# Four in-order instruction streams of a chunk of a selective scan, laid out in another order

## The chip, the cores and the metric

One Trainium2 chip, one NeuronCore of it. The metric is the device time of one execution in microseconds (us); smaller is better. Before the change it is 11698.7 us, the median of 3 runs (11697.71 to 11724.16).

## The reference

A batch of 8 images (96 channels, 64x64) goes through a Mamba-like block with a convolutional branch, then through linear attention and a quantised feed-forward layer. The part that matters here is the selective scan, over 4 directions `k`, 192 channels `d` and 16 states `n`, along the 4096 positions of an image:

```python
x_dbl = jnp.einsum('bkdl,kcd->bkcl', xs, x_proj_w)
dts, bs, cs = (x_dbl[:, :, :R], x_dbl[:, :, R:R + N], x_dbl[:, :, R + N:])
dts = jnp.einsum('bkrl,kdr->bkdl', dts, dt_projs_w)
delta = jax.nn.softplus(dts + dt_projs_b[None, :, :, None])
...
dA = jnp.exp(dt_i[..., None] * A)
hst = dA * hst + (dt_i * u_i)[..., None] * b_i[:, :, None, :]
y = jnp.einsum('bkdn,bkn->bkd', hst, c_i)
```

## The kernel before

Three phases run one after the other: `phase_inputs` (line 70), `phase_scan` (line 379) and `phase_outputs` (line 1163). The change is in `phase_scan` alone.

**Tiling.** The scan walks 8 images x 4 directions x 4 chunks of 1024 positions: 128 chunks. The 192 x 16 states of a chunk are 24 tiles of 128 partitions x 1024 positions, numbered 0 to 23 (`i` in the code). For each tile, four things happen:

- ScalarE makes the decay, exp(A * delta), with `expo` (line 893). It reads `rep`, delta copied to 128 partitions.
- The drive, delta * u * B, comes from one of two places. For 18 tiles GpSimd multiplies it (`drive`, line 1108) into a ring of four buffers `dBu`; a drive has a number of its own, `place(i)`, from 0 to 17. For the 6 "turned" tiles 9 to 14 ScalarE scales delta * u, turned so that positions lie on partitions (`scale_du`, line 934, 32 small steps in a chunk), and TensorE turns it back (`turn_back`, line 799, 8 blocks of 128x128).
- VectorE runs the recurrence (`scan`, line 1068). 16 tiles ("kept") are scanned into one of 8 buffers `h`; the other 8 (0, 3, 4, 6, 15, 18, 19, 21) are scanned in place in the PSUM buffer `pd`.
- The states are multiplied by C: kept tiles by GpSimd (`weigh`, line 1116), the others by VectorE (`weigh`, line 1077). TensorE then sums three tiles at a time into `py` (`reduce_states` j sums tiles 3j to 3j+2, line 821). After groups 0 to 3 ScalarE copies the first half of y out of `py` (`copy_y(n, 0)`, line 968), and after groups 4 to 7 the second half (`copy_y(n, 1)`). The first sum of the next half waits for that copy.

Beside this, the chunk's delta and delta * u of the next chunk are made, in two halves of 96 channels: TensorE's `make_step` (L767), ScalarE's `absolute`, `exp_abs`, `relu`, `one_plus`, `log` (L940 to L958), TensorE's `add_up` (L775 to L780), which adds up the four parts of softplus, ScalarE's `copy_delta` (L963), VectorE's `delta_u` (L1049), TensorE's `turn_du` (L787) and ScalarE's `copy_du` (L921). For the chunk after the next, TensorE's `make_x_dbl` (L749) and `turn_b` (L757) and ScalarE's `copy_x_dbl` (L910) and `copy_b` (L914) make B and C. All of these share one PSUM buffer, `pp`.

**What sets the order.** Every engine runs its own list, in order, written out by hand: `body` for TensorE, VectorE and GpSimd, and on ScalarE `run` (line 1000), which goes through steps i = 0 to 23. At each step it saves the last column of a state for the next chunk (`save_state`, L901), issues `expo(i + 2)`, and then what the tables `STEPS`, `SCALE` (scaling steps of this chunk) and `SCALE_NEXT` (of the next one) put there. `copy_y` and `copy_x_dbl` have their steps in the code. A `pd` buffer is free for `expo(i)` when tile i - 2 has been scanned, or, if it is scanned in place, weighed. SP's list of DMAs waits for semaphores of all four engines.

Of the kernel before, what the change touches and what calls it, by code (L numbers as in the profile page):

```python
# [378 lines left out]
def phase_scan(nc, a):  # L379

    with ExitStack() as ctx:
# [358 lines left out]
        def _(pe):  # L740
# [95 lines left out]

            def body(bk, k, c, left):
                n, s = bk * NC + c, c % 2
                reduce_states(n, k, 0)
                if left:  # L840
                    add_up(n + 1, 0)
                turn_back(bk, c, 9)
                turn_back(bk, c, 10)
                reduce_states(n, k, 1)
                turn_back(bk, c, 11)
                turn_back(bk, c, 12)
                if left:
                    turn_du(n + 1, 0)
                turn_back(bk, c, 13)
                if left:  # L850
                    make_step(n + 1, 1)
                turn_back(bk, c, 14)
                skip(n, s, 0)
                reduce_states(n, k, 2)
                reduce_states(n, k, 3)
                reduce_states(n, k, 4)
                if left:
                    add_up(n + 1, 1)
                skip(n, s, 1)
                if left:  # L860
                    turn_du(n + 1, 1)
                reduce_states(n, k, 5)
                if left >= 2:
                    make_x_dbl(n + 2, s)
                    turn_b(n + 2)
                    make_step(n + 2, 0)
                reduce_states(n, k, 6)
                reduce_states(n, k, 7)
# [3 lines left out]
        def _(act):  # L872
# [107 lines left out]
            for i in range(2):  # L980
# [4 lines left out]

            STEPS = {1: [(absolute, 0)],
                     2: [(exp_abs, 0), (relu, 0), (one_plus, 0)],
                     4: [(log, 0)],
                     8: [(copy_delta, 0)],
                     11: [(copy_du, 0)],  # L990
                     12: [(absolute, 1), (exp_abs, 1)],
                     13: [(relu, 1)],
                     14: [(one_plus, 1)],
                     16: [(log, 1)],
                     18: [(copy_delta, 1)],
                     20: [(copy_du, 1)]}
            SCALE = {0: 3, 2: 2, 3: 3, 4: 2, 5: 6, 6: 2, 7: 1}
            SCALE_NEXT = {20: 5, 21: 3, 22: 2, 23: 3}

            def run(bk, k, c, left, first, span):  # L1000
                n, s = bk * NC + c, c % 2
                for i in span:
                    if c < NC - 1:
                        for q in range(NS):
                            if SAVED_AT[q] == i:
                                save_state(bk, k, c, q)
                    if i + 2 < NS:
                        expo(bk, k, c, i + 2)
                    elif left:
                        if c == NC - 1 and i + 2 == NS:  # L1010
                            pick_a(bk + 1, (k + 1) % K)
                        expo(*((bk, k, c + 1) if c < NC - 1 else (bk + 1, (k + 1) % K, 0)), i + 2 - NS)
                    if i == 2 and not first:
                        copy_y(n - 1, 1)
                    if i == 14:
                        copy_y(n, 0)
                    if left:
                        for step, half in STEPS.get(i, ()):
                            step(n + 1, half)
                        if left >= 2 and i == 22:  # L1020
                            copy_x_dbl(n + 2)
                        if left >= 2 and i == 23:
                            copy_b(n + 2, s)
                    if i in SCALE:
                        made = AHEAD + sum(SCALE[q] for q in SCALE if q < i)
                        scale_du(n, s, made, made + SCALE[i])
                    if left and i in SCALE_NEXT:
                        made = sum(SCALE_NEXT[q] for q in SCALE_NEXT if q < i)
                        scale_du(n + 1, 1 - s, made, made + SCALE_NEXT[i])

# [10 lines left out]
        def _(dve):  # L1041
# [43 lines left out]
            def body(bk, k, c, left):  # L1085
                n, s = bk * NC + c, c % 2
                for j in range(8):
                    for i in range(3 * j, 3 * j + 3):
                        scan(bk, k, c, i)
                        if not is_kept(i):  # L1090
                            weigh(n, i)
                        if left and i in (10, 20):
                            delta_u(n + 1, 1 - s, (10, 20).index(i))
            chunk_loop(dve, body)

        @block.gpsimd
        def _(pool):
# [24 lines left out]
            def body(bk, k, c, left):  # L1122
                n = bk * NC + c
                drive(n, c, 3)
                drive(n, c, 4)
                weigh(n, k, 1)
                weigh(n, k, 2)
                drive(n, c, 5)
                drive(n, c, 6)
                drive(n, c, 7)  # L1130
                drive(n, c, 8)
# [11 lines left out]
                weigh(n, k, 14)  # L1143
                drive(n, c, 12)
                drive(n, c, 13)
                weigh(n, k, 16)
                weigh(n, k, 17)
                drive(n, c, 14)
                drive(n, c, 15)
                drive(n, c, 16)  # L1150
                drive(n, c, 17)
# [759 lines left out]
```

## Time and profile before

| | |
|---|---|
| median of 3 runs | 11698.7 us |
| the profiled execution: its own time | 11687.62 us |
| span of the profile, first to last instruction | 11685.8 us |
| `phase_scan`, about 838 to 10117 us of the span | 9279 us, 128 chunks |
| the chunk that is read below, from its first scan to that of the next | 5050.18 to 5122.46 us, 72.28 us |
| mean granted TensorE clock | 0.871 of 2.4 GHz |
| busy share of the whole span | TensorE 79%, VectorE 86%, ScalarE 72%, GpSimd 75% |

In the rows, PE is TensorE (PEld its weight loads), DVE is VectorE, ACT is ScalarE, POOL is GpSimd and SP the DMA queue's engine. A row of a timeline has a start, a duration, the engine, the line of the kernel, the operation and its tiles; "xN" is a run of N like instructions, "[idle before <-releaser]" how long the engine stood idle ahead of it and which event ended that. Lines are those of the kernel before; in the kernel after they are the same up to the table `STEPS` (line 986) and lie one lower behind it.

### The profile page before, as it was taken

Reading aid. Unit: us, or ns where it says so; the run is one execution under the profiler, and the core shown is the slowest. Engines: PE = TensorE matmul, PEld = TensorE weight load, DVE = VectorE, ACT = ScalarE, POOL = GpSimd, SP = SyncE. Lnnn points to the kernel's source line nnn. Section 1 sums busy time; section 2 is a strip of 40 time slices with the busy share of each in tenths; the row PEclk is TensorE's granted clock in tenths of the full one; section 3 lists DMA queues with packets and bytes.
Section 4 is the critical chain, followed back from the end, with each engine's and each line's share of the span. In section 5 each row is a group of like instructions: output and inputs, shape, how many; then the busy total and the mean of one; then the engine's idle time right before and its main releaser. Section 6 shows DMA issues by size and latency. Waiting matters only on the chain. (4 is left out here: it accounts for less than half of the span.)

```text
span 11685.8 us, 144402 instructions
## 1 busy us (share of the span) xinstructions
PE 9207.4 (79%) x34584; PEld 3443.5 (29%) x34584; DVE 10036.1 (86%) x6335; ACT 8437.5 (72%) x13829; POOL 8772.1 (75%) x4468
## 2 busy tenths in 40 slices
PE   8877777777777777777777777777777777588888
PEld 2322222222222222222222222222222222233333
DVE  7759999999899989999999899999999999866565
ACT  6767777777777777777777777777777777455555
POOL 0019999899899989999999899999999999521210
PEclk9988888888888888888888888888888888799999
DMA  3347777787777777777777777777777777643441
GB/s 103 122 127 185 183 187 184 178 187 186 183 180 185 187 183 181 186 187 183 184 185 188 179 183 185 185 182 181 185 186 184 187 186 182 149 112 94 100 108 49
DMA packets 577596, 1948.45 MB, mean 167 GB/s; under 512 B 106614, under 2 KB 111638, under 8 KB 562198
## 3 DMA queue, kind: packets, MB, share of 16 engines
q1 hardware_dynamic: 573714, 1938.65, 69.8%
q8 instruction: 272, 4.46, 0.2%
q14 instruction: 534, 4.37, 0.1%
q10 hardware_dynamic: 3076, 0.97, 0.1%
HBM read 1532.38 MB, written 406.85 MB: 166 GB/s over the span
## 5 line engine op out<-in xcount | busy, mean ns | idle before, releaser
L1108 POOL TENSOR_TENSOR dBu<-rep,shared 128x1024 f32<-128x1024 f32 x2304 | 4552.5, 1998 | 886.2 <-DMA rep<-dd_dram 833.5
L1116 POOL TENSOR_TENSOR h<-h,shared 128x1024 f32<-128x1024 f32 x2048 | 4020.7, 1972 | 728.6 <-DVE h L1068 728.0
L893 ACT ACTIVATE pd<-rep,a_now 128x1024 f32<-128x1024 f32 x2304 | 2556.1, 1109 | 362.7 <-DVE h L1068 200.9
L821 PE MATMUL py<-h,fold 128*32 128x512 f32 x8192 | 2447.8, 701 | 214.9 <-ACT y L968 214.9
L1068 DVE TENSOR_TENSOR_SCAN h<-pd,carry,dBu 128x1024 f32<-128x1024 f32 x960 | 2242.4, 2344 | 409.7 <-ACT pd L893 280.0
L1068 DVE TENSOR_TENSOR_SCAN pd<-pd,carry,dBu 128x1024 f32<-128x1024 f32 x768 | 1795.8, 2338 | 0.1
L821 PE MATMUL py<-shared,fold 128*32 128x512 f32 x3072 | 1479.6, 880 | 221.8 <-ACT y L968 173.3
L934 ACT ACTIVATE shared<-shared,turned_b 128x192 f32<-128x192 f32 x4096 | 1553.2, 442 | 15.5 <-ACT shared L921 5.4
L799 PE MATMUL pd<-eye,shared 128*128 128x128 f32 x6144 | 1006.9, 316 | 619.3 <-DVE h L1068 466.9
L1068 DVE TENSOR_TENSOR_SCAN h<-h,carry,pd 128x1024 f32<-128x1024 f32 x576 | 1308.8, 2326 | 43.2 <-PE pd L799 32.3
L799 PEld LDWEIGHTS pd<-eye,shared 128*128 128x128 f32 x6144 | 792.8, 159 | 1083.4 <-DVE h L1068 478.0
L1077 DVE TENSOR_TENSOR shared<-pd,shared 128x1024 f32<-128x1024 f32 x768 | 940.5, 1225 | 87.8 <-DVE pd L1068 26.0
L893 ACT ACTIVATE h<-rep,a_now 128x1024 f32<-128x1024 f32 x768 | 867.4, 1140 | 1.2 <-PE py L821 1.2
L1068 DVE TENSOR_TENSOR_SCAN h<-pd,dBu 128x1024 f32<-128x1024 f32 x320 | 729.2, 2284 | 139.5 <-ACT pd L893 88.7
L1813 POOL TENSOR_TENSOR shared<-shared 96x1024 f32<-96x1024 f32 x56 | 139.2, 2516 | 938.9 <-DMA shared<-y_dram 938.9
L767 PE MATMUL pp<-xdbl,w_dt 38*96 38x512 f32 x1024 | 716.8, 836 | 152.0 <-ACT turned_b L914 151.1
L787 PE MATMUL pp<-eye,RL 96*128 96x96 f32 x2048 | 298.1, 307 | 559.5 <-DVE RL L1049 554.5
L821 PEld LDWEIGHTS py<-h,fold 128*32 128x32 f32 x8192 | 484.4, 124 | 567.3 <-issue 531.4
L1068 DVE TENSOR_TENSOR_SCAN pd<-pd,dBu 128x1024 f32<-128x1024 f32 x256 | 585.4, 2287 | 66.0 <-ACT pd L893 50.2
L775 PE MATMUL pp<-W,neg 97*96 97x512 f32 x1024 | 545.5, 614 | 106.5 <-ACT W L953 106.5
L921 ACT ACTIVATE shared<-pp 128x768 f32<-128x768 f32 x256 | 207.5, 810 | 571.1 <-PE pp L787 571.1
L968 ACT ACTIVATE y<-py 96x1024 f32<-96x1024 f32 x256 | 260.7, 1019 | 473.1 <-PE py L821 473.0
(174 smaller groups left out, 14120.2 us busy)
## 6 DMA issues: line engine op xcount, KB each, us to landing
rep<-dd_dram SPq DMA_DIRECT2D x1024, 768.0 KB, 13.0
shared<-bc_dram SPq DMA_DIRECT2D x3584, 128.0 KB, 4.6
u<-u_dram SPq DMA_DIRECT2D x128, 768.0 KB, 6.8
dd_dram<-LG SPq DMA_DIRECT2D x256, 384.0 KB, 4.0
dd_dram<-RL SPq DMA_DIRECT2D x256, 384.0 KB, 5.1
y_dram<-y SPq DMA_DIRECT2D x256, 384.0 KB, 8.1
shared<-y_dram SPq DMA_DIRECT2D x63, 1536.0 KB, 15.7
u_dram<-shared SPq DMA_DIRECT2D x32, 1536.0 KB, 7.5
```

Of the source, the lines that this page charges most:

```text
L767: last = mm(pp[0:HALF, t2(t)], w_dt[:, half * HALF:(half + 1) * HALF], xdbl[:, t2(t)], start=True, stop=True)
L775: mm(pp[0:HALF, t2(t)], neg[:, :], W1[:, t2(t)], start=True, stop=False)
L787: last = nc.tensor.transpose(pp[:, q * 128:q * 128 + HALF], du[:, block_of(q)], eye)
L799: last = nc.tensor.transpose(pd[:, i % 2, block_of(q)], turned_dbu[:, q, half * 3 + g, :, :], eye128[:, :])
L821: last = mm(py[32 * g:32 * g + 32, t2(t)], fold[:, :], weighted(3 * j + g, k)[:, t2(t)], start=(j % 4 == 0), stop=(j % 4 == 3), skip_group ...
L893: go(dst, rep[:, half, 0, g, :], ACT.Exp, scale=a_now[:, column(i)]).then_inc(S.exped, 1)
L934: go(turned_dbu[:, q, :, j, :], turned_du[:, q, :, :], ACT.Identity, scale=turned_b[:, s, q, j:j + 1]).then_inc(S.scaled, 1)
L968: go(y[:, :], py[0:HALF, :], ACT.Identity).then_inc(S.y_made, 1)
L1068: v.tensor_tensor_scan(turned(state(i, k), k), turned(decay, k), turned(drive, k), first, ALU.mult, ALU.add).then_inc(S.scanned, 1)
L1077: v.tensor_tensor(weighted(i, 0), pd[:, i % 2, :], CC[:, r, :], ALU.mult).then_inc(S.hc_dve, 1)
L1108: nc.gpsimd.tensor_tensor(dBu[:, ring(c, p), :], rep[:, half, 1, g, :], BB[:, r, :], ALU.mult).then_inc(S.dbu, 1)
L1116: nc.gpsimd.tensor_tensor(turned(weighted(i, k), k), turned(kept(i, k), k), turned(CC[:, r, :], k), ALU.mult).then_inc(S.hc_pool, 1)
```

## The change

Nothing is added or removed: the same instructions with the same waits stand in another order on TensorE, ScalarE, VectorE and GpSimd.

```diff
@@ body of TensorE
                 n, s = bk * NC + c, c % 2
-                reduce_states(n, k, 0)
                 if left:
                     add_up(n + 1, 0)
                 turn_back(bk, c, 9)
+                reduce_states(n, k, 0)
                 turn_back(bk, c, 10)
+                turn_back(bk, c, 11)
                 reduce_states(n, k, 1)
-                turn_back(bk, c, 11)
-                turn_back(bk, c, 12)
                 if left:
                     turn_du(n + 1, 0)
+                turn_back(bk, c, 12)
                 turn_back(bk, c, 13)
...
                 reduce_states(n, k, 3)
-                reduce_states(n, k, 4)
                 if left:
                     add_up(n + 1, 1)
+                reduce_states(n, k, 4)
                 skip(n, s, 1)
@@ ScalarE
             STEPS = {1: [(absolute, 0)],
                      2: [(exp_abs, 0), (relu, 0), (one_plus, 0)],
-                     4: [(log, 0)],
-                     8: [(copy_delta, 0)],
+                     5: [(log, 0)],
+                     7: [(copy_delta, 0)],
                      11: [(copy_du, 0)],
-                     12: [(absolute, 1), (exp_abs, 1)],
-                     13: [(relu, 1)],
-                     14: [(one_plus, 1)],
-                     16: [(log, 1)],
+                     12: [(absolute, 1)],
+                     13: [(exp_abs, 1), (relu, 1), (one_plus, 1)],
+                     15: [(log, 1)],
                      18: [(copy_delta, 1)],
                      20: [(copy_du, 1)]}
-            SCALE = {0: 3, 2: 2, 3: 3, 4: 2, 5: 6, 6: 2, 7: 1}
-            SCALE_NEXT = {20: 5, 21: 3, 22: 2, 23: 3}
+            SCALE = {0: 3, 1: 1, 2: 3, 3: 1, 4: 2, 5: 5, 6: 4}
+            SCALE_NEXT = {20: 3, 21: 2, 22: 4, 23: 4}
...
-                    if i == 2 and not first:
+                    if i == 4 and not first:
                         copy_y(n - 1, 1)
-                    if i == 14:
+                    if i == 16:
                         copy_y(n, 0)
...
-                        if left >= 2 and i == 22:
+                        if left >= 2 and i == 23:
                             copy_x_dbl(n + 2)
@@ body of VectorE
-                        if left and i in (10, 20):
-                            delta_u(n + 1, 1 - s, (10, 20).index(i))
+                        if left and i in (9, 20):
+                            delta_u(n + 1, 1 - s, (9, 20).index(i))
@@ body of GpSimd
                 drive(n, c, 3)
+                weigh(n, k, 1)
                 drive(n, c, 4)
-                weigh(n, k, 1)
+                drive(n, c, 5)
                 weigh(n, k, 2)
-                drive(n, c, 5)
...
                 drive(n, c, 13)
+                drive(n, c, 14)
                 weigh(n, k, 16)
                 weigh(n, k, 17)
-                drive(n, c, 14)
```

Three places, as the two programs have them. First ScalarE in steps 2 to 4 of a chunk. Before, the copy of y (L968) stands between the exponential of tile 4, just above these rows, and that of tile 5 (the last row):

```order
L967 ISA
L968 ACTIVATE y<-py 96x1024
L944 ACTIVATE E<-E 96x1024
L947 ISA
L949 ACTIVATE RL<-pp,b_dt 96x1024
L953 ACTIVATE W<-E 96x1024
L934 ACTIVATE shared<-shared,turned_b 128x6x32 x2
L901 ACTIVATE carry<-h 128x1
L900 REGISTER_ALU
L901 ACTIVATE carry<-pd 128x1
L903 REGISTER_ALU
L893 ACTIVATE pd<-rep,a_now 128x1024
```

Now, from the first save of step 3 on (L893 is the exponential of tile 5, then that of tile 6):

```order
L900 REGISTER_ALU
L901 ACTIVATE carry<-pd 128x1
L903 REGISTER_ALU
L893 ACTIVATE pd<-rep,a_now 128x1024
L934 ACTIVATE shared<-shared,turned_b 128x6x32
L901 ACTIVATE carry<-h 128x1
L900 REGISTER_ALU
L901 ACTIVATE carry<-pd 128x1
L903 REGISTER_ALU
L893 ACTIVATE pd<-rep,a_now 128x1024
L967 ISA
L968 ACTIVATE y<-py 96x1024
```

The copy of y has moved behind the exponentials of tiles 5 and 6, and one scaling step more (L934) stands ahead of tile 5's.

Second, ScalarE where one chunk passes into the next (L893 is the exponential of the next chunk's tile 0, then that of its tile 1; L901 saves states). Before:

```order
L893 ACTIVATE pd<-rep,a_now 128x1024
L906 REGISTER_ALU
L907 ISA
L908 ISA
L910 ACTIVATE xdbl<-pp 38x1024
L934 ACTIVATE shared<-shared,turned_b 128x6x32 x2
L901 ACTIVATE carry<-h 128x1
L898 REGISTER_ALU
L901 ACTIVATE carry<-h 128x1
L893 ACTIVATE pd<-rep,a_now 128x1024
L914 ACTIVATE turned_b<-pp 128x32
L933 REGISTER_ALU
```

Now:

```order
L893 ACTIVATE pd<-rep,a_now 128x1024
L934 ACTIVATE shared<-shared,turned_b 128x6x32
L933 ISA
L934 ACTIVATE shared<-shared,turned_b 128x6x32 x3
L901 ACTIVATE carry<-h 128x1
L898 REGISTER_ALU
L901 ACTIVATE carry<-h 128x1
L893 ACTIVATE pd<-rep,a_now 128x1024
L906 REGISTER_ALU
L907 ISA
L908 ISA
L910 ACTIVATE xdbl<-pp 38x1024
```

The copy of x_dbl (L910) has moved behind tile 1's exponential, with four scaling steps ahead of that instead of two.

Third, TensorE between turn 9 (the last of its eight blocks is the first row) and group 1's sum. Before, with group 0's sum done earlier still, ahead of `add_up`:

```order
L799 MATMUL pd<-eye,shared 128x128
L793 REGISTER_ALU
L799 MATMUL pd<-eye,shared 128x128 x8
L818 REGISTER_ALU x2
L816 REGISTER_ALU
L821 MATMUL py<-shared,fold 32x512 x2
L821 MATMUL py<-h,fold 32x512
L821 MATMUL py<-shared,fold 32x512 x2
L821 MATMUL py<-h,fold 32x512
L793 REGISTER_ALU
L799 MATMUL pd<-eye,shared 128x128 x8
```

Now:

```order
L799 MATMUL pd<-eye,shared 128x128
L818 ISA
L816 ISA
L816 REGISTER_ALU
L821 MATMUL py<-shared,fold 32x512
L821 MATMUL py<-h,fold 32x512 x2
L821 MATMUL py<-shared,fold 32x512
L821 MATMUL py<-h,fold 32x512 x2
L793 REGISTER_ALU
L799 MATMUL pd<-eye,shared 128x128 x8
L793 REGISTER_ALU
L799 MATMUL pd<-eye,shared 128x128 x8
```

Group 0's sum now stands between turns 9 and 10, and turn 11 follows turn 10 ahead of group 1's sum.

## Rows read from the trace of the kernel before

**Rows 1.** Busy time by stretch: PE, PEld, DVE, ACT, POOL, clock, DMA.

```profile
5050.18:5122.46 72.28, 56.81 (x226) 21.56 (x224) 66.82 (x35) 55.66 (x98) 66.02 (x35) 0.86 0.79 186
...
5077.30:5085.00 7.70, 7.50 (x31) 4.01 (x32) 7.60 (x4) 7.22 (x13) 7.70 (x5) 0.56 0.34 93
5085.00:5095.00 10.00, 9.10 (x57) 5.36 (x57) 9.63 (x6) 5.68 (x8) 7.78 (x5) 1.00 0.72 171
...
838.00:10117.00 9279.00, 7198.57 (x28587) 2709.70 (x28585) 8492.41 (x4350) 7032.94 (x11789) 8497.67 (x4350) 0.86 0.78 183
```

**Rows 2.** What VectorE waited for, 3000 to 7000 us: total, times, longest.

```profile
DVE h L1068 <- ACT pd L893: 148.8, 103, 4.3
DVE h L1068 <- POOL dBu L1108: 58.0, 34, 3.6
DVE pd L1068 <- ACT pd L893: 37.1, 7, 7.7
```

**Rows 3.** Timeline of VectorE, 5050 to 5122.5 us.

```profile
5047.91 2.35 DVE L1068 TENSOR_TENSOR_SCAN h<-pd,carry,dBu 128x1024 f32<-128x1024 f32 x1 [0.33 <-ACT pd L893]
...
5054.30 4.69 DVE L1068 TENSOR_TENSOR_SCAN h<-pd,carry,dBu 128x1024 f32<-128x1024 f32 x2 [0.33 <-ACT pd L893]
...
5068.99 2.35 DVE L1068 TENSOR_TENSOR_SCAN h<-pd,carry,dBu 128x1024 f32<-128x1024 f32 x1 [2.88 <-ACT pd L893]
...
5085.81 9.06 DVE L1068 TENSOR_TENSOR_SCAN h<-h,carry,pd 128x1024 f32<-128x1024 f32 x4 [0.37 <-PE pd L799]
...
5101.25 2.35 DVE L1068 TENSOR_TENSOR_SCAN h<-pd,carry,dBu 128x1024 f32<-128x1024 f32 x1 [0.52 <-ACT carry L901]
...
5120.20 2.35 DVE L1068 TENSOR_TENSOR_SCAN h<-pd,carry,dBu 128x1024 f32<-128x1024 f32 x1 [0.33 <-ACT pd L893]
```

**Rows 4.** Timeline of ScalarE, 5045 to 5125 us.

```profile
5051.02 1.02 ACT L910 ACTIVATE xdbl<-pp 38x1024 f32<-38x1024 f32 x1 [1.31 <-PE pp L749]
...
5052.82 1.10 ACT L893 ACTIVATE pd<-rep,a_now 128x1024 f32<-128x1024 f32 x1
5053.86 0.18 ACT L914 ACTIVATE turned_b<-pp 128x32 f32<-128x32 f32 x1
...
5055.16 1.12 ACT L893 ACTIVATE pd<-rep,a_now 128x1024 f32<-128x1024 f32 x1
...
5059.28 1.10 ACT L893 ACTIVATE pd<-rep,a_now 128x1024 f32<-128x1024 f32 x1
5062.72 1.02 ACT L968 ACTIVATE y<-py 96x1024 f32<-96x1024 f32 x1 [2.34 <-PE py L821]
5063.64 1.04 ACT L944 ACTIVATE E<-E 96x1024 f32<-96x1024 f32 x1
...
5067.51 1.12 ACT L893 ACTIVATE pd<-rep,a_now 128x1024 f32<-128x1024 f32 x1
```

**Rows 5.** Timeline of TensorE, 5046 to 5122.5 us.

```profile
5052.18 0.66 PE L757 MATMUL pp<-eye,xdbl 38*128 38x38 f32 x8 [1.41 <-ACT xdbl L910]
...
5061.99 0.59 PE L821 MATMUL py<-h,fold 128*32 128x512 f32 x2
...
5072.02 1.96 PE L780 MATMUL pp<-LG,eye 96*96 96x512 f32 x4
5077.33 1.75 PE L799 MATMUL pd<-eye,shared 128*128 128x128 f32 x7 [3.35 <-DVE h L1068]
5079.23 2.46 PE L799 MATMUL pd<-eye,shared 128*128 128x128 f32 x9
5081.62 1.07 PE L821 MATMUL py<-shared,fold 128*32 128x512 f32 x2
...
5082.48 1.07 PE L821 MATMUL py<-shared,fold 128*32 128x512 f32 x2
...
5088.21 1.09 PE L799 MATMUL pd<-eye,shared 128*128 128x128 f32 x8 [0.90 <-DVE h L1068]
```

**Rows 6.** Timeline of GpSimd, 5045 to 5122.5 us.

```profile
5061.14 7.89 POOL L1108 TENSOR_TENSOR dBu<-rep,shared 128x1024 f32<-128x1024 f32 x4
```

## The prediction

> **What bounds the kernel now.** I read four views in this order. First the busy time by stretch, to see which engine is near its limit in the scan phase. It lasts 9279 us for 128 chunks, 72.5 us each, and VectorE and GpSimd are busy in 8492 and 8498 us of it, that is 66.3 and 66.4 us a chunk; in the chunk that I walk through, 66.82 and 66.02 of 72.28 us [rows 1]. TensorE and ScalarE have over 15 us of room. So no engine is full: two engines at 92% stand still some 6 us a chunk, and each of these waits can only be repaired by what ends it.
>
> Second, what VectorE waited for between 3000 and 7000 us, which is 55 chunks: most of it goes to the exponentials on ScalarE, 148.8 + 37.1 us, and 58.0 us are put down to GpSimd's drives [rows 2]. The second name is not to be trusted: a wait for several semaphores goes to the one whose last update came latest, whoever it was for. The timeline tells more. In the chunk from 5050.18 us VectorE has one long stall, 2.88 us ahead of tile 5, and short ones of 0.33 (tile 1), 0.37 (tile 11), 0.52 (tile 17) and 0.33 us (tile 23) [rows 3]; the other 1.0 us are small hand-overs, as from a scan in PSUM to its own product, which no order changes. (The row from 5054.30 us holds the scans of tiles 1 and 2, 2.25 us apart.)
>
> Third, why tile 5 waits. ScalarE made tile 4's exponential at 5059.28, then waited 2.34 us for TensorE with the copy of y's second half, did it at 5062.72, then three parts of softplus and two scaling steps, and came to tile 5's exponential at 5067.51; the scan began 1.48 us behind that start, just as tile 1's scan began 1.48 us behind its own (5052.82 and 5054.30) [rows 3, 4]. Nothing on VectorE's side needed the copy at that moment: the exponentials are queued behind it because ScalarE runs its list in order.
>
> Fourth, TensorE: it finished group 7's sum at 5062.58 (5061.99 + 0.59), which released the copy [rows 5].
>
> **The change part by part.** Times are from the first scan of a chunk, t = 0 at 5050.18.
>
> *The copy of y's second half behind tile 6's exponential.* It leaves the path to tile 5 with its wait and its own 0.92 us (5062.72 to 5063.64). At its new place, about t = 18, group 7 has been summed for 5 us, so it waits for nothing. Who waits for it: group 0's sum on TensorE, which is moved behind `add_up` and turn 9 for that, and SP's store of y.
>
> *The chunk's start.* The copy of x_dbl moves from in front of tile 1's exponential to behind it. That exponential needs the scan of tile 23, over at t = 0.08 (5047.91 + 2.35) [rows 3], and can start at about 0.8, when ScalarE has done four scaling steps behind tile 0's exponential, instead of 2.64. Tile 1 then loses its stall of 0.33: its scan starts at 3.8. But the copy of x_dbl starts at 0.8 + 1.03 = 1.85, 1.0 later than before. The turn of B starts 1.16 behind that and takes 0.66 [rows 4, 5], so the copy of B comes at 3.9 instead of 3.68. Between it and tile 2's exponential there were three scaling steps and 1.30 us; now there are four, at 0.35 each (3 of them took 1.13 with an overlap): 5.5 instead of 4.98. Tile 2 is scanned at 5.5 + 1.48 = 7.0; before it was 6.37, right behind tile 1. So this part costs 0.6 us at tile 2, between 0 (if the copy of B is ready early) and 1.2 (if TensorE's x_dbl is late by as much again).
>
> *Up to tile 5.* From tile 2's exponential to tile 4's it was 4.10 us; with one scaling step more 4.47: t = 10.0. Then, without the copy, 1.03 for itself and 3.87 + 0.35 for what stood between 5063.64 and 5067.51, again with one scaling step more: tile 5's exponential at 15.2, its scan at 16.7. VectorE itself gets there 9.56 us behind tile 2's scan (5056.55 to 5068.99, less the stall of 2.88), at 16.6, so a stall of about 0.1 is left of 2.88. The scan stood at 18.81: **2.1 us gained**, with 0.6 of loss already in it.
>
> *Tiles 6 to 9.* The log (step 5), five and four scaling steps stand between the exponentials of tiles 7, 8 and 9. Added up at the same paces, tile 8's is just in time and tile 9's 0.35 late. I take **0.35 lost**, between 0 and 0.7.
>
> *Turns ahead of sums, and delta * u after tile 9.* Turn 9 needs the last scaling step, which comes at about 9.3 us behind tile 5's scan. So it ends at 26.3, and group 0's sum, four rounds that start 0.43 apart at the full clock, at 28.2. Turn 10 ends at 29.4. Tile 10 needs it at 30.8, since delta * u (1.12 us) now stands ahead of tile 10 and covers it: 1.1 us of margin with 0.3 for the hand-over. Turn 11 follows as soon as tile 9 is scanned, so the 0.37 us at tile 11 go. Turn 12 now stands behind group 1 and the turn of delta * u and has 0.1 to 0.3 us of margin at the full clock. **0.37 gained**; the lower end is the third rival below.
>
> *The copy of y's first half behind tile 18's exponential:* tile 17 no longer waits for a save and an exponential queued behind it. **0.52 gained**. Ahead of tile 23's exponential five scaling steps become three, 0.7 us, so its stall of 0.33 goes. **0.33 gained**.
>
> *At nothing.* `add_up` of the second half ahead of group 4's sum: both lie in TensorE's room. GpSimd's product of tile 1 ahead of drive 4 makes it idle about 1 us (drive 3 is over at 5.2, tile 1 is scanned at 6.1), but drive 4 is still ready at about 10 for a scan at 12.9. Drive 14 two places earlier has its ring buffer by then and lets SP load B and u earlier. If this cover is gone, the price is that of the fourth rival.
>
> Sum for this chunk: 2.1 - 0.35 + 0.37 + 0.52 + 0.33 = 2.97, so 3.0 us of 72.28. Over 128 chunks 384 us; the phases before and after are untouched. Against the profiled execution's own 11687.6 us that is 11304 us; the median of the runs is 11 us above it, so I forecast **11310 us**. A measurement of this kernel can tell about 0.3%, 35 us or 0.27 us a chunk, from no change.
>
> **A rule against it.** The rows show both clocks around the turns: a mean of 0.56 of 2.4 GHz, nearly all at 1.2, in the 7.7 us that begin with turns 9 and 10 after 3.35 us without work, and 1.00 in the next 10 us with turns 11 to 14 [rows 1, 5]. The Trainium skill ("TensorE: Matmul & The Clock Gate", Part 4, PE-mode transpose) says that the high clock does not engage for transposes, which don't count as work in the same way. By that rule a stretch with more turns in a row would stay at 1.2 GHz, and the third or fifth rival would come out. In the trace turns 11 to 14 ran at the full clock between other matmuls, so I give the rule a small part. The Trainium skill ("GPSIMD Engine Reference", Key points) also says that GpSimd contends with VectorE's instructions of two SBUF inputs; that would make it slower as VectorE's gaps close. The row says no: four drives took 7.89 us, 1.97 each, though VectorE stood idle in 2.88 us of them [rows 3, 6], and over the phase its 4350 instructions take 1.95 us each [rows 1].
>
> **The rivals.**
>
> *Second, the chunk's start costs nothing* (chance 0.11). ScalarE catches up, and the stalls go with no new ones at tiles 2 and 9: 2.88 + 0.33 + 0.37 + 0.52 + 0.33 = 4.4, less 0.3 for hand-overs, 4.1 us: 525 us, 11175. For it: the sum of ScalarE's work is the same and it has 16 us of room. Against: the copy of x_dbl hangs on TensorE's late end.
>
> *Third, TensorE is late at turn 10* (0.16). If the slow stretch still begins at turn 9 and lasts as long as now, group 0's sum takes 1.7 us more (rounds 0.86 apart instead of 0.43) and turn 10 1.1 more (2.2 against 1.09) [rows 5]; less the 1.1 of margin, tile 10 stalls 1.7 us. The gain is 1.3 us: 166 us, 11530. For it: this stretch was slow in the chunk shown. Against: the idle time ahead of turn 9, after the last part of `add_up` (5072.02), shrinks from 3.35 us to about 1.3, since the log moves back towards it.
>
> *Fourth, GpSimd becomes the bound* (0.05). It needs 66.0 us itself; of its 6.26 us of idle time the part that stems from VectorE's stall of 2.88 goes, 0.9 us come in ahead of tile 1's product, and if all the rest binds, the chunk takes 72.28 - 2.88 + 0.9 = 70.3 us: 2.0 us gained, 256 in all, 11440.
>
> *Fifth, slower* (0.05). The clock stays at 1.2 GHz from group 0's sum through turn 12. Two sums at 1.7 and three turns at 1.1 us more are 6.7 us; less 0.2 of margin at turn 12, VectorE stalls 6.5 us between tiles 10 and 12, which outweighs the gain of 3.0 by 3.5: 448 us, 12145. It decides from 3.2 us of lateness at turn 12 on, that is when the slow stretch outlasts turn 11. [...]
>
> *Sixth, the change doesn't do what it says* (0.03): the stall stays with the copy at its new step, because group 7's sum slides back as well: within 0.3% of 11699. It would have to slide 5 us.
>
> **How the numbers follow.** Forecast 0.60, the others as given. Faster by over 0.3%: 0.60 + 0.11 + 0.16 + 0.05 = 0.92; within: 0.03; slower: 0.05. The ends: with the start's cost at 0 and tile 9's at 0 the gain is 4.0 to 4.1 us, 11170; with 1.2 at tile 2 and half of the third rival's stall it is 2.97 - 0.6 - 0.85 = 1.5 us, 11510.
>
> **What would show it.** Chunks of about 69.3 us; tile 5's stall down from 2.9 to under 0.5 us; no wait of the copy of y's second half for TensorE; a new stall of about 1 us at tile 2 and a short one at tile 9; none at tiles 11, 17, 23; GpSimd's wait ahead of tile 5's product gone. I am wrong if VectorE stalls at tiles 10 to 12 behind turns, if GpSimd has no idle time left, or if chunks stay over 71.

## The result, and the profile after

| | before | after |
|---|---|---|
| median of 4 runs each, same chip | 11702.44 us | **11232.64 us** (11205.89 to 11255.03) |
| ratio | | **0.9594** (95%: 0.957 to 0.9619) |
| profiled execution, its own time | 11687.62 us | 11255.03 us |
| mean granted TensorE clock | 0.871 | 0.864 |

The change makes the kernel 470 us faster, 3.67 us a chunk. The forecast was 11310 us (388 us, 3.0 a chunk) in a range of 11170 to 11510.

Busy time by stretch, after (PE, PEld, DVE, ACT, POOL, clock, DMA share, GB/s). The first row is a chunk from its first scan to that of the next, the second the whole scan phase, then 4000 us in the middle (58 chunks, 55 in the kernel before), and two short stretches around turns 9 to 12:

```profile
5396.20:5464.29 68.09, 56.47 (x224) 20.88 (x222) 66.49 (x36) 55.74 (x100) 66.68 (x35) 0.85 0.83 190
839.00:9650.00 8811.00, 7241.98 (x28588) 2649.50 (x28586) 8453.70 (x4350) 7048.51 (x11790) 8488.62 (x4349) 0.86 0.83 193
3000.00:7000.00 4000.00, 3303.83 (x12984) 1206.50 (x12984) 3829.76 (x1972) 3197.82 (x5341) 3849.55 (x1972) 0.86 0.84 193
5421.00:5425.00 4.00, 4.00 (x21) 1.97 (x19) 3.95 (x2) 4.00 (x9) 4.00 (x3) 0.60 0.00 0
5425.00:5437.00 12.00, 11.73 (x74) 6.64 (x74) 12.00 (x7) 7.79 (x12) 12.00 (x7) 1.00 0.63 168
```

The gain lies in the scan phase: 9279 us [rows 1] became 8811, 468 us less. VectorE's idle time in that phase fell from 787 to 357 us (span less busy time), that is from 6.15 to 2.79 us a chunk. The other 39 us, 0.30 a chunk, come out of its busy time at the same 4350 instructions: back-to-back instructions overlap by some 0.1 us (a row "4.58 ... x2" holds two scans of 2.35), and more of them stand back to back now. The profiled execution as a whole is only 433 us shorter than the one before, since its output phase, which no edit touches, took 1603 us and not 1569 (1571 to 1593 in the other runs' traces). So that the medians differ by 470 us, nearly the scan phase's 468, is in part chance.

What VectorE waited for, 3000 to 7000 us, after (total, times, longest; before: [rows 2]):

```profile
DVE h L1067 <- ACT pd L893: 58.0, 62, 5.5
DVE hC L1076 <- DMA shared<-bc_dram: 12.0, 18, 1.4
DVE h L1067 <- PE pd L799: 11.3, 22, 1.1
DVE h L1067 <- POOL dBu L1107: 7.3, 11, 4.3
DVE pd L1067 <- ACT pd L893: 2.1, 4, 0.7
```

The waits for exponentials fell from 185.9 to 60.1 us, those put down to the drives from 58.0 to 9.1 (a row of 1.8 for `pd` is not shown), those for ScalarE's saves (`carry`, L901) from 24.0 to 2.3. GpSimd's drives had not become faster (1998 ns each before, 2000 after, over 2304 of them), so that name was indeed the wrong one. Nor do they run slower beside a VectorE that is busy in 96% of the time instead of 91 (3829.76 and 3649.02 of these 4000 us). The Trainium skill ("GPSIMD Engine Reference", Key points) tells of contention with VectorE's instructions of two SBUF inputs. It does not bear on this kernel, and the prediction was wrong to hold it against the row: every scan and product of VectorE reads one of its two large inputs from `pd` or `pp`, which lie in PSUM. So no run here tests that rule.

Timeline of VectorE, after, in the chunk from 5396.20 us (tile 2; tile 3's product; tile 5; tile 9; delta * u; tiles 10 to 14; tiles 16 and 17; tile 18):

```profile
5402.73 2.35 DVE L1067 TENSOR_TENSOR_SCAN h<-pd,carry,dBu 128x1024 f32<-128x1024 f32 x1 [0.47 <-ACT pd L893]
...
5407.45 1.22 DVE L1076 TENSOR_TENSOR shared<-pd,shared 128x1024 f32<-128x1024 f32 x1
...
5412.45 2.35 DVE L1067 TENSOR_TENSOR_SCAN h<-pd,carry,dBu 128x1024 f32<-128x1024 f32 x1 [0.24 <-POOL dBu L1107]
...
5423.05 2.35 DVE L1067 TENSOR_TENSOR_SCAN h<-h,carry,pd 128x1024 f32<-128x1024 f32 x1
5425.31 1.20 DVE L1048 TENSOR_TENSOR RL<-pp,u 96x1024 f32<-96x1024 f32 x1
5426.47 11.30 DVE L1067 TENSOR_TENSOR_SCAN h<-h,carry,pd 128x1024 f32<-128x1024 f32 x5
...
5441.28 4.58 DVE L1067 TENSOR_TENSOR_SCAN h<-pd,carry,dBu 128x1024 f32<-128x1024 f32 x2
5445.78 2.33 DVE L1067 TENSOR_TENSOR_SCAN pd<-pd,carry,dBu 128x1024 f32<-128x1024 f32 x1
```

Tile 5 waits 0.24 us where it waited 2.88 [rows 3], and its scan starts at t = 16.25 where it started at 18.81. Tile 2 has the new stall of the forecast, here 0.47. There is nothing at tiles 9, 11 and 17. GpSimd's wait ahead of tile 5's product is gone as forecast: 2.30 us on average before, 0.24 after.

ScalarE in the same chunk (copy of x_dbl, copy of B, exponentials of tiles 2 and 5, copies of y's second and first half):

```profile
5397.74 1.00 ACT L910 ACTIVATE xdbl<-pp 38x1024 f32<-38x1024 f32 x1
...
5399.59 0.20 ACT L914 ACTIVATE turned_b<-pp 128x32 f32<-128x32 f32 x1 [0.84 <-PE pp L757]
...
5401.25 1.12 ACT L893 ACTIVATE pd<-rep,a_now 128x1024 f32<-128x1024 f32 x1
...
5410.97 1.12 ACT L893 ACTIVATE pd<-rep,a_now 128x1024 f32<-128x1024 f32 x1
...
5413.69 1.00 ACT L968 ACTIVATE y<-py 96x1024 f32<-96x1024 f32 x1
...
5444.73 1.00 ACT L968 ACTIVATE y<-py 96x1024 f32<-96x1024 f32 x1
```

Neither copy of y waits; the second half's copy had waited 2.34 us [rows 4]. Nor does TensorE wait for a copy of y any more, where it had waited 176.5 us between 3000 and 7000 us. Against t = 0 at 5396.20, the copy of x_dbl starts at 1.54 (forecast 1.85), the copy of B at 3.39 (3.9) and tile 2's exponential at 5.05 (5.5). The copy of B waits 0.84 us for TensorE's turn, with nothing between it and the copy of x_dbl.

TensorE: turn 9 (8 blocks), the first and last round of group 0's sum, turns 10 and 11 (16 blocks):

```profile
5420.95 1.92 PE L799 MATMUL pd<-eye,shared 128*128 128x128 f32 x8
...
5422.80 1.07 PE L821 MATMUL py<-h,fold 128*32 128x512 f32 x2
...
5424.81 0.59 PE L821 MATMUL py<-h,fold 128*32 128x512 f32 x2
5425.34 1.97 PE L799 MATMUL pd<-eye,shared 128*128 128x128 f32 x16
```

Turn 9 took 1.92 us at a clock near 1.2 GHz; turns 10 and 11, eight blocks each, took 1.97 together at the granted clock of 1.00. The Trainium skill ("TensorE: Matmul & The Clock Gate", Part 4, PE-mode transpose) says that the high clock does not engage for transposes; the trace does not agree, as far as these 16 go, which ran at it behind a sum that had already risen to it (its first rounds 0.86 apart, its last 0.43). Whether a stretch of nothing but transposes would rise to it no run shows.

Some chunks, most of them the second of a direction (13 of the 14 of chunks 16 to 111 whose tile 2 waits over 2 us), have a long stall. TensorE, ScalarE and VectorE in the one from 5042.92 us (timeline of all engines):

```profile
5042.22 6.86 PE L749 MATMUL pp<-u,w_x 96*38 96x512 f32 x8 [2.69 <-DMA u<-u_dram]
...
5049.34 1.02 ACT L910 ACTIVATE xdbl<-pp 38x1024 f32<-38x1024 f32 x1 [4.62 <-PE pp L749]
...
5054.33 2.35 DVE L1067 TENSOR_TENSOR_SCAN h<-pd,carry,dBu 128x1024 f32<-128x1024 f32 x1 [5.38 <-ACT pd L893]
```

The load of u was issued at 5030.77 and let TensorE start 11.4 us later; it had stood 2.69 us, made x_dbl at 1.2 GHz (6.86 us, where it takes 3.65 in the chunk above), the copy of x_dbl waited 4.62 us and tile 2 was scanned 5.38 us late.

### The profile page after: what moved, and what is told of

Same layout as the page of the kernel before. It is cut to its first block and busy times, and to the rows that moved or that the text cites. A ratio compares the mean times of both kernels' runs of the same rounds, so it can differ in the third digit from the quotient of the medians.

```text
span 11253.2 us, 144402 instructions
## 1 busy us (share of the span) xinstructions
PE 9276.6 (82%) x34584; PEld 3385.5 (30%) x34584; DVE 10007.4 (89%) x6335; ACT 8454.9 (75%) x13829; POOL 8763.8 (78%) x4468
## 5 line engine op out<-in xcount | busy, mean ns | idle before, releaser
L893 ACT ACTIVATE pd<-rep,a_now 128x1024 f32<-128x1024 f32 x2304 | 2560.4, 1111 | 395.4 <-DVE h L1067 198.3
L821 PE MATMUL py<-h,fold 128*32 128x512 f32 x8192 | 2472.6, 720 | 6.0 <-ACT y L968 6.0
L934 ACT ACTIVATE shared<-shared,turned_b 128x192 f32<-128x192 f32 x4096 | 1552.6, 442 | 15.6 <-ACT shared L921 5.4
L821 PE MATMUL py<-shared,fold 128*32 128x512 f32 x3072 | 1457.0, 839 | 5.3 <-POOL h L1115 4.3
L799 PE MATMUL pd<-eye,shared 128*128 128x128 f32 x6144 | 903.7, 296 | 178.0 <-DVE h L1067 127.4
L799 PEld LDWEIGHTS pd<-eye,shared 128*128 128x128 f32 x6144 | 734.6, 150 | 618.7 <-DVE h L1067 341.2
L893 ACT ACTIVATE h<-rep,a_now 128x1024 f32<-128x1024 f32 x768 | 866.4, 1140 | 16.1 <-PE py L821 15.3
L780 PE MATMUL pp<-LG,eye 96*96 96x512 f32 x1024 | 598.7, 715 | 228.9 <-ACT LG L958 228.8
L767 PE MATMUL pp<-xdbl,w_dt 38*96 38x512 f32 x1024 | 641.3, 757 | 37.6 <-ACT turned_b L914 36.7
L749 PE MATMUL pp<-u,w_x 96*38 96x512 f32 x1024 | 521.1, 656 | 90.8 <-DMA u<-u_dram 79.5
```

What stands on the lines that cost most here:

```text
L749: last = mm(pp[0:XD, t2(t)], w_x[:, half, :], u[:, s, half, t2(t)], start=(half == 0), stop=(half == 1))
L767: last = mm(pp[0:HALF, t2(t)], w_dt[:, half * HALF:(half + 1) * HALF], xdbl[:, t2(t)], start=True, stop=True)
L780: last = mm(pp[0:HALF, t2(t)], eye, LG[:, t2(t)], start=False, stop=True)
L799: last = nc.tensor.transpose(pd[:, i % 2, block_of(q)], turned_dbu[:, q, half * 3 + g, :, :], eye128[:, :])
L821: last = mm(py[32 * g:32 * g + 32, t2(t)], fold[:, :], weighted(3 * j + g, k)[:, t2(t)], start=(j % 4 == 0), stop=(j % 4 == 3), skip_group ...
L893: go(dst, rep[:, half, 0, g, :], ACT.Exp, scale=a_now[:, column(i)]).then_inc(S.exped, 1)
```

## The experiments

Below, "mean idle" is the idle time ahead of an instruction averaged over 96 chunks of a run's trace (chunks 16 to 111), so it answers for more than one timeline does; the length of a chunk is the mean over the first 126. For the kernels before and after:

| mean idle ahead of, us | tile 1 | tile 2 | tile 5 | tile 9 | tile 10 | tile 11 | tile 15 | tile 17 | tile 23 | all of VectorE | chunk |
|---|---|---|---|---|---|---|---|---|---|---|---|
| before | 0.50 | 0.01 | 3.01 | 0.09 | 0.00 | 0.33 | 0.39 | 0.44 | 0.26 | 6.32 | 72.54 |
| after | 0.00 | 0.98 | 0.20 | 0.05 | 0.14 | 0.00 | 0.03 | 0.00 | 0.00 | 2.87 | 68.85 |

My theory: the gain comes from the copy of y's second half, which no longer holds up ScalarE's exponentials. The rival: it comes from TensorE's order, and the copies matter little. Ratios are to the kernel before on the same chip; after is 0.959.

**y2_back**: after, with this copy at its old step. The rest of the change stays, so this run also shows what the rest is worth without the late copy.

```diff
-                    if i == 4 and not first:
+                    if i == 2 and not first:
                         copy_y(n - 1, 1)
```

> The kernel after with one part undone: the copy of y's second half stands at step 2 again, in front of the exponentials of tiles 5 and 6. Theory (ScalarE's list queues tile 5's exponential behind a copy that waits for group 7's sum): the copy waits some 2 us again and takes 0.9, tile 5 stalls 2.9 to 3.2 us instead of 0.2, the chunk gets 2.9 us longer, 11600 us (ratio to before 0.991). Rival (ScalarE's spare time swallows the copy wherever it stands, the gain came from the turns and sums on TensorE): under 1 us a chunk, 11350 us or less.

Measured 11485.21 us, 0.9806 (0.979 to 0.9823), chunks of 70.83 us. Tile 5's mean idle is 3.09 again and the copy waits 1.92. But the small waits at tiles 2, 6 and 10 shrink, so that the copy's place is worth 2.0 us a chunk and not the 2.9 that tile 5 waits longer: VectorE's stall had served as slack for others. The time lies between what the theory (11600) and the rival (11350 or less) foretold: with the copy at its old step the rest of the change still gives 1.9% of the 4.1.

**y2_alone**: before, with nothing changed but this copy (step 2 to 4).

> The kernel before with the copy of y's second half at step 4, and nothing else. Theory (the other parts of the change are there to make room for the late copy): group 0's sum, first in TensorE's list, waits for the copy until about t = 18 and holds up add_up, turn 9 and copy_delta behind it; tile 5's stall goes, but 1 to 2 us come back at tiles 9 to 12, so the gain is 1 to 2 us a chunk, 11450 to 11570 us. Rival (the copy alone carries the gain): 2.9 us a chunk or more, 11330 us or less.

Measured 12034.43 us, **1.0271** (1.0254 to 1.0289): slower than before. Tile 5's stall is gone (0.01), and 3.83 us stand ahead of tile 9, 1.57 ahead of tile 17. TensorE in this run, the first rows of group 0's sum and `add_up`, then turns 9 and 10; behind them tile 9's scan on VectorE:

```profile
5528.49 1.06 PE L821 MATMUL py<-shared,fold 128*32 128x512 f32 x1 [6.20 <-ACT y L968]
...
5532.06 1.91 PE L775 MATMUL pp<-W,neg 97*96 97x512 f32 x2
...
5539.82 1.91 PE L799 MATMUL pd<-eye,shared 128*128 128x128 f32 x16
```

```profile
5540.90 4.58 DVE L1068 TENSOR_TENSOR_SCAN h<-h,carry,pd 128x1024 f32<-128x1024 f32 x2 [3.72 <-PE pd L799]
```

The copy ran at 5527.17, and group 0's sum, first in TensorE's old order, had to wait for it: 6.20 us idle. The sum then took 3.6 us (rounds 0.85 apart, the 1.2 GHz pace), `add_up` stands behind it and turn 9 behind that. In the waits between 3000 and 7000 us, TensorE's wait for the copies grew from 176.5 us in the kernel before to 408.4. Both had this kernel faster and neither was right: the copy and TensorE's order are one edit.

**pe_back**: after, with TensorE's whole list of before.

> The kernel after with TensorE's list of before (group 0's sum first, sums of groups 0, 1 and 4 ahead of turns and of add_up). Theory: group 0's sum waits for the copy of y until t = 18, add_up ends at 27 instead of 24.5, turn 9 at 29, tiles 9 and 11 stall 1 to 2 us together, 11360 to 11490 us. Rival (TensorE has 15 us of room in a chunk, its order does not matter): 11233 us within 35.

Measured 12265.18 us, **1.0475** (1.0457 to 1.0492), 775 us over what was expected. Tile 9 waits 3.89 us, delta * u after tile 20 waits 2.72, tile 2 1.64; TensorE's wait for the copies is 609.8 us. The next two runs split this.

**g0_back**: after, with group 0's sum alone back at the head of the list.

```diff
+                reduce_states(n, k, 0)
                 if left:
                     add_up(n + 1, 0)
                 turn_back(bk, c, 9)
-                reduce_states(n, k, 0)
```

> The kernel after with group 0's sum first in TensorE's list again, ahead of add_up, and nothing else undone. Theory (the sum waits for the late copy of y, TensorE stands idle and falls to 1.2 GHz, and add_up, turn 9 and the copy of delta queue behind it): tile 9 stalls about 4 us as with the whole list of before, 4 us a chunk, 11700 to 11800 us. Rival (the stall at tile 9 came from the order of turns and sums after turn 9): under 1 us a chunk, 11350 us or less.

Measured 11655.48 us, 0.9976 (0.9966 to 0.9987), a little under the 11700 to 11800 expected. The stall is the one foretold, tile 9 waits 3.74 us, but the small waits at tile 2, tile 10 and the product of tile 6 shrink by 0.6 together, so the chunk gets 3.5 us longer and not 4. So nearly all of the change's gain hangs on whether group 0's sum stands behind `add_up` and turn 9, once the copy is late. TensorE in the chunk from 5317.17 us, the start of that sum and turns 9 and 10:

```profile
5336.40 1.06 PE L821 MATMUL py<-shared,fold 128*32 128x512 f32 x1 [5.58 <-ACT y L968]
...
5346.89 1.91 PE L799 MATMUL pd<-eye,shared 128*128 128x128 f32 x16
```

**g4_back**: after, with group 4's sum alone back ahead of `add_up` of the second half.

```diff
                 reduce_states(n, k, 3)
+                reduce_states(n, k, 4)
                 if left:
                     add_up(n + 1, 1)
-                reduce_states(n, k, 4)
```

> The kernel after with group 4's sum ahead of the second add_up again, and nothing else undone. Theory (the sum waits for the copy of y's first half, which now stands at step 16; add_up, the copy of delta and delta * u queue behind it): a stall of 1.5 to 3 us ahead of the second delta * u, 11430 to 11600 us. Rival (TensorE has slack there, as the prediction costed it at nothing): 11233 us within 35.

Measured 11934.82 us, **1.0207** (1.0183 to 1.0231), far over the expectation. Rows of one chunk; TensorE's group 4, its x_dbl; ScalarE's copy of delta; SP's load of u; VectorE's delta * u and, in the next chunk, tile 2:

```profile
5381.57 3.38 PE L821 MATMUL py<-h,fold 128*32 128x512 f32 x12 [5.42 <-ACT y L968]
...
5400.08 5.32 PE L749 MATMUL pp<-u,w_x 96*38 96x512 f32 x8 [2.81 <-DMA u<-u_dram]
```

```profile
5392.04 1.02 ACT L963 ACTIVATE LG<-pp 96x1024 f32<-96x1024 f32 x1 [5.88 <-PE pp L780]
```

```profile
5393.96 0.33 SPq L618 DMA_DIRECT2D u<-u_dram  x1
```

```profile
5393.20 1.22 DVE L1048 TENSOR_TENSOR RL<-pp,u 96x1024 f32<-96x1024 f32 x1 [2.74 <-ACT LG L963]
...
5410.65 2.35 DVE L1067 TENSOR_TENSOR_SCAN h<-pd,carry,dBu 128x1024 f32<-128x1024 f32 x1 [2.29 <-ACT pd L893]
```

The sum waits for the copy of y's first half, 5.42 us, and runs at the 1.2 GHz pace, 3.38 us. It then strikes twice. `add_up` is late, so delta is, and VectorE waits with delta * u. And `skip`, the last reader of u, is late, so SP loads the next u late, TensorE waits 2.81 us for it and makes x_dbl in 5.32 us, and tile 2 of the next chunk is late. I had counted the first strike, at 1.5 to 3 us, and not the second. Mean idle: 3.51 us at delta * u, 2.89 at tile 2.

**xdbl_back**: after, with the copy of x_dbl back at step 22 (ahead of tile 1's exponential).

> The kernel after with the copy of x_dbl at step 22 again, in front of the exponential of the next chunk's tile 1 (scaling steps as after). Theory: that exponential waits for TensorE's x_dbl and for four scaling steps, tile 1 stalls about 1.5 to 2 us, tile 2's stall of 1.0 shrinks by a part, net 0.5 to 1.4 us a chunk, 11300 to 11410 us. Rival (only the time of the copy of B counts, and that comes as early or earlier): no change or faster, 11233 us within 35 or less.

Measured 11408.25 us, 0.9743 (0.9727 to 0.976), at the upper end of what was expected. Tile 2's mean idle falls from 0.98 to 0.27, but tile 1's is 1.82, and chunks take 70.08 us. The new place is worth 1.2 us a chunk beside the new table of scaling steps, which puts four of them ahead of tile 1's exponential and which this run keeps. That does not contradict the forecast's loss of 0.6 for the chunk's start, which was against the kernel before: there tile 2 was scanned at 6.56 on average, with the whole change at 6.99, in this run at 8.20.

**pool_back**: after, with GpSimd's list of before.

> The kernel after with GpSimd's list of before (drive 4 ahead of tile 1's product, drive 5 behind tile 2's, drive 14 behind the products of tiles 16 and 17). Theory (GpSimd has 2 us of idle time in a chunk and every drive is ready 2 us early): 11233 us within 35. Rival (drive 14 frees B's buffer for SP's loads and, behind them, the load of u, so x_dbl and tile 2 come later): 0.5 us a chunk or more, 11300 us or more; or the reverse, loads less bunched with u's, and faster by 35 us or more.

Measured 11214.68 us, 0.9599 (0.9583 to 0.9616): no difference from after, as expected. But the loads change, see the last section.

**y1_back**: after, with the copy of y's first half at its old step 14.

> The kernel after, with the copy of y's first half back at step 14 (behind tile 16's exponential) instead of 16. By my forecast's term for it, tile 17's stall returns: 0.5 us a chunk, 65 us, ratio 0.965. The run g4_back showed that groups 3 and 4 and the copy hang together: with the copy two steps earlier it waits for the sum of group 3 (in the kernel before 1.0 us on average), and as ScalarE is then also late for the exponentials of tiles 17 to 19, the price may be 1 us a chunk: 0.970. A rival: group 4's sum, which waits for this copy, stands behind add_up now and comes later anyway, so nothing changes: 0.959.

Measured 11218.56 us, 0.9602 (0.9585 to 0.962): no difference, as the rival had it, though for another reason. The copy did not wait, 0.06 us on average where in the kernel before it waited 1.01. TensorE sums groups 2 and 3 earlier now, against the chunk's first scan: group 3's last round ends at 44.7 us on average and in the kernel before at 47.4, while ScalarE comes to the copy only 1.8 us earlier. So tile 17's stall goes by either edit: with the copy back it is 0.04, and with TensorE's old order and the copy at step 16 (pe_back, g0_back) it is 0.00.

Then three attempts at a version that is faster still. **after_again** runs after beside them.

> The kernel after, once more beside the other three: 0.959 of the time before.

Measured 11206.8 us, 0.9588 (0.9575 to 0.9601). The same program gives other waits in this trace than in the one above: 51.5 us for exponentials instead of 60.1, and in a direction's second chunk 1.58 us at tile 2 instead of 2.51. So a change of waits of that size, between two traces, says nothing.

**fill**: after, with two scaling steps of step 23 between the copy of x_dbl and the copy of B, in the 0.84 us in which ScalarE waits for TensorE's turn.

```diff
-            SCALE_NEXT = {20: 3, 21: 2, 22: 4, 23: 4}
+            SCALE_NEXT = {20: 3, 21: 2, 22: 5, 23: 3}
...
+                        if i == 23:
+                            scale_du(n + 1, 1 - s, 10, 12)
                         if left >= 2 and i == 23:
                             copy_b(n + 2, s)
```

> The kernel after with the scaling steps around the copies of x_dbl and B laid out anew: one more ahead of tile 1's exponential, two between the copy of x_dbl and the copy of B (where ScalarE waits 0.9 us for the turn of B), one behind it instead of four. Theory (tile 2's stall of 1.0 us hangs on the 1.0 us of scaling steps between the copy of B and tile 2's exponential): tile 2's exponential comes 0.9 us earlier, the stall shrinks to about 0.4 (what is left stems from late loads of u), 0.5 to 0.8 us a chunk, 11130 to 11170 us. Rival (tile 2's stall is all late x_dbl): under 0.2 us a chunk, 11210 us or more.

Measured 11206.27 us, 0.9592 (0.9573 to 0.961): nothing. What VectorE waited for, 3000 to 7000 us, in this run:

```profile
DVE h L1069 <- ACT pd L893: 28.6, 32, 3.3
DVE h L1069 <- PE pd L799: 25.3, 38, 1.4
DVE hC L1078 <- DMA shared<-bc_dram: 20.1, 20, 2.3
DVE shared L1078 <- PE py L821: 17.0, 26, 1.2
```

Against the kernel after, the exponentials' waits in the first row are halved, by 29.4 us (6.3 more stand ahead of scans in place, 8.4 instead of 2.1), and 14.0 came in at the turns, 8.1 at products that wait for a load of C, and 17.0 at a product that overwrites a buffer which TensorE's sum of group 6 still reads (a wait that the list of the kernel after does not have).

**u_first**: after, with SP's load of u ahead of four copies of C.

```diff
                     load_b(n + 1, 1 - s, 1)
-                    load_c(n + 1, 1 - s, 0)
                     if left >= 2:
                         load_u(bk, k, c + 2, s)
+                    load_c(n + 1, 1 - s, 0)
```

> The kernel after, with SP's load of u for the chunk after the next issued ahead of the four copies of C (row 0) instead of behind them. If the long stall at tile 2 in every fourth chunk (5.4 us in the one read) comes from a load of u that lands behind those copies and makes x_dbl late, the mean stall at tile 2 falls from 1.0 to 0.5 us and the time by 0.5 x 128 = 60 us, to a ratio of 0.954. If the load is late because the transfer itself is slow in a crowd of others, nothing changes: 0.959.

Measured 11212.05 us, 0.9589 (0.9575 to 0.9604): nothing. The cause that I named is real, but it doesn't pay. Against after_again, TensorE's wait for u fell from 17.8 us to 5.4, tile 2's mean idle in the second chunk of a direction from 1.58 to 0.89. Rows of the same view as above, in this run:

```profile
DVE h L1067 <- ACT pd L893: 43.5, 70, 3.4
DVE h L1067 <- PE pd L799: 23.4, 40, 1.4
DVE hC L1076 <- DMA shared<-bc_dram: 20.2, 23, 2.0
```

The row of exponentials is 43.5 (58.0 in after, 49.7 in after_again), the turns are at 23.4 (11.3 and 9.0) and the load of C at 20.2 (12.0 and 11.9): what the first row lost the others took.

**u_fill**: both edits.

> u_first together with the scaling steps of the run fill (two of them between the copy of x_dbl and the copy of B). fill halved VectorE's waits for exponentials and lost as much in products that wait for TensorE's sums of groups 6 and 7. If those sums were late because x_dbl was late, both gains hold now: 0.950. If they are late because make_step (3.7 us at 1.2 GHz) stands ahead of them, the same as u_first.

Measured 11216.2 us, 0.9596 (0.9581 to 0.961). Waits for exponentials are at 14.3 us, and the load of C at 39.7. VectorE's busy time from 3000 to 7000 us differs no more between these programs than between two traces of one: 3829.76 us of 4000 in after and 3845.45 in after_again, 3828.73 in fill, 3829.03 in u_first, 3836.61 in u_fill. What holds the chunk at 68.7 us once tile 2 is repaired is not settled: GpSimd is busy in 96% of the stretch (3849.55 us), the loads of C land late and TensorE runs part of each chunk at 1.2 GHz. Of these, pool_back takes away most of the wait for the loads of C (4.5 us instead of 12.0), without a gain, but it leaves tile 2's stall (0.84); no run takes away the other two. No version beat the kernel after by more than the measurement tells.

## Why the prediction was right

The sign, the mechanism and most of the size came out; the time is 77 us under the forecast, well inside the range. By its steps:

- **Tile 5, 2.1 us with the chunk's start in it: right, a little small.** The scan stands at 16.61 on average, 16.7 forecast; in the kernel before it stood at 19.02 on average and at 18.81 in the chunk that I walked, so 2.4 were gained. y2_back shows that the stall is the copy's. One reading was off: the scans of tiles 1 and 2 are 2.34 us apart and not 2.25 (the row from 5054.30 holds two of 2.35 in 4.69), so that 0.2 and not 0.1 should have been left of the stall, and 0.20 is. It did not enter the sum.
- **The chunk's start, 0.6 lost: right in the sum, too high in the chunk read.** Tile 2 has 0.47 us there and 0.98 on average, forecast 1.0; but the average is made of some 0.5 in most chunks and long stalls where the load of u is late. That the load could be the cause was not in the prediction.
- **Tile 9, 0.35 lost: wrong.** Its mean idle is 0.05. ScalarE ran ahead of my count from the copy of x_dbl on, by 0.3 to 0.5 us in the chunk above, and 0.35 was all that I had it late by.
- **Tiles 11, 17, 23: right**, 0.33, 0.44 and 0.26 us on average where I had read 0.37, 0.52 and 0.33. But the reason given for tile 17 was one of two that each suffice (y1_back). For tile 11, that turn 11 comes earlier is argued and not shown: no run moves it alone. For tile 23, its stall stays where ScalarE's tables are the old ones (0.27 in y2_alone) and is gone where they are the new ones (pe_back), which fits.
- **Not in the sum:** tile 15's idle of 0.39 went to 0.03, it is not in the chunk that I walked, and why it went no run shows (it is back, at 0.37 to 0.41, in pe_back, g0_back and g4_back); and 0.30 us a chunk of overlap between instructions that now stand back to back. Against that, 0.4 us came in at the product of tile 6 (0.17), tile 10 (0.14) and tile 16 (0.12).
- **The walked chunk was a good one:** 5.46 us of idle time on VectorE, where the phase has 6.15 on average. Both numbers stood in [rows 1]. Tile 9, tile 15 and the overlap are 0.4, 0.36 and 0.3 us; less the 0.4 they make the 0.7 us a chunk that were missing. (Tile 5's 0.3 more and the 0.2 less at tiles 11, 17 and 23 nearly cancel.) So the time came as close as it did by luck in part: errors of 0.3 to 0.4 us stand on both sides of the sum.
- **"At nothing" was right as a forecast of this change and misleading as a price.** GpSimd's list is worth nothing (pool_back). But `add_up` ahead of group 4's sum is worth 5.6 us a chunk as soon as the copy stands at step 16 (g4_back), and group 0's move 3.5 (g0_back). "Both lie in TensorE's room" looked at TensorE's mean load, 79%, where the question was which of its instructions waits for a copy, and what is queued behind it.
- **Not undone by any run:** ScalarE's new tables and delta * u behind tile 9 as such. y2_back still holds them together with TensorE's new order, and how its 1.9% divides among them is open.
- **The rivals.** The second had tile 9 right and failed at tile 2; its time, 11175, is 58 us off and the forecast 77, so the time alone does not decide between them, tile 2's 0.98 us does. The third (turn 10 late) and fifth (slow clock through turn 12) failed: turns 10 to 12 ran at the full clock in the chunk shown, and tile 10 waits 0.14 us on average. Their mechanism is what g0_back and y2_alone show, at tile 9 and not at tile 10. The fourth: GpSimd had 8811 less 8488.62 us idle, 2.5 us a chunk, so it is close but did not bind by more than that.

## What to carry to other kernels

When an instruction is moved later on one in-order engine, ask which engine waits for it and what is queued behind that waiter: here the copy of y alone made the kernel 2.7% slower, and the same copy, with the waiting sums moved behind ready work and the rest of the change, made it 4% faster. Price such edits as pairs. When several chains are within half a microsecond of each other, as in the last three attempts here, repairing one of them returned nothing, and the table of waits told why: the total stays and the names change. And compare two traces of one program before a change of waits is believed.

## What was not expected of the hardware

- After 5 to 6 us without work TensorE's first sum ran at the 1.2 GHz pace: group 4's sum in g4_back took 3.38 us after 5.42 idle, where the same twelve matmuls took 1.92 in the kernel after, without a wait. So such a late release cost TensorE some 1.5 us more than the wait itself.
- In the kernel after, a transfer takes longer from its issue to its landing, and this is not because more bytes move (193 GB/s against 183 from 3000 to 7000 us): the order of GpSimd's list does it. The DMA issues, with the size of each and the median us from issue to landing, in the kernel before, in the kernel after and in pool_back:

```profile
shared<-bc_dram SPq DMA_DIRECT2D x1540, 128.0 KB, 4.6
u<-u_dram SPq DMA_DIRECT2D x55, 768.0 KB, 6.7
```

```profile
shared<-bc_dram SPq DMA_DIRECT2D x1624, 128.0 KB, 7.2
u<-u_dram SPq DMA_DIRECT2D x58, 768.0 KB, 9.3
```

```profile
shared<-bc_dram SPq DMA_DIRECT2D x1624, 128.0 KB, 4.7
u<-u_dram SPq DMA_DIRECT2D x58, 768.0 KB, 6.7
```

pool_back moves 193 GB/s too and has the short times. What differs is the issue: u is issued 55.8 us behind the chunk's first scan in the kernel after and 58.3 in pool_back (medians), and lands at 65.3 and 65.0. So the earlier issue, which the prediction hoped drive 14 would bring, brought u no earlier. With the four copies of C issued behind it (u_first) u lands at 63.5, 7.8 us after its issue. Why the earlier issue gained nothing is not shown beyond that.
